# One-hot matrices of the edge stage made by GpSimd and ScalarE in place of VectorE

## What is computed

```python
def _tconv(x, src, dst, edge_attr, ...):
    q, k, v = x @ Wq + bq, x @ Wk + bk, x @ Wv + bv      # (n, H=4, C=64)
    e = edge_attr @ We
    kj, vj = k[src] + e, v[src] + e
    logits = einsum('ehc,ehc->eh', q[dst], kj) / sqrt(C)
    m = segment_max(logits, dst)
    ex = exp(logits - m[dst])
    a = ex / (segment_sum(ex, dst)[dst] + 1e-16)
    return segment_sum(vj * a[:, :, None], dst) + x @ Ws + bs
```

## Time and profile before

| | |
|---|---|
| median of 3 runs | 5051.55 us (5050.83 to 5053.5) |
| profiled execution, its own time | 5044.08 us |
| its span in the trace | 5042.3 us |
| mean granted TensorE clock | 0.933 |
| busy share PE, DVE, ACT, POOL | 83%, 76%, 54%, 54% |
| `edges`, first gather of layer 1 to last of layer 2 | 470.7 to 4046.1 us |

### The profile page before, as it was taken

How to read it: one execution, slowest core, us unless ns; L and a number is a source line. 1 busy time by engine, 2 the same in 40 slices (tenths; PEclk the granted TensorE clock), 3 DMA queues, 4 the chain that set the end, 5 groups by cost and what they waited for, 6 DMA issues and landing times. The chain is left out here.

```text
span 5042.3 us, 107396 instructions
## 1 busy us (share of the span) xinstructions
PE 4191.8 (83%) x19200; PEld 3376.1 (67%) x19201; DVE 3851.4 (76%) x8465; ACT 2724.1 (54%) x10172; POOL 2738.1 (54%) x2848
## 2 busy tenths in 40 slices
PE   2986999999999999978899999999999943049960
PEld 1555888788778788733688878877877833049960
DVE  3444999999999999955799999999999977202222
ACT  0120677777777777731477777767777741013320
POOL 1011777667667677500677767766767723442235
PEclk9998999999999999999999999999999975579985
DMA  4457877777777777534877777777777723522235
GB/s 85 138 195 225 235 215 215 212 216 215 209 212 216 209 217 216 170 118 143 233 219 215 217 209 215 213 210 212 217 213 214 216 74 104 175 94 70 71 95 152
DMA packets 616287, 920.13 MB, mean 182 GB/s; under 512 B 114501, under 2 KB 477829, under 8 KB 615558
## 3 DMA queue, kind: packets, MB, share of 16 engines
q0 software_dynamic: 154448, 501.87, 34.8%
q1 hardware_dynamic: 378390, 323.25, 22.5%
q10 hardware_dynamic: 82848, 88.64, 4.9%
HBM read 800.89 MB, written 112.53 MB: 181 GB/s over the span
## 5 line engine op out<-in xcount | busy, mean ns | idle before, releaser
L870 POOL DMA_INDIRECT edge_kv<-kvD,edge_ix x1760 | 1821.9, 1035 | 961.9 <-issue 556.5
L909 ACT ACTIVATE edge_w<-edge_vj,edge_ex 128x64 f32<-128x64 f32 x7040 | 1872.0, 340 | 647.3 <-PE edge_pa L950 377.1
L927 PE MATMUL edge_ps<-edge_We,edge_ea 112*128 112x256 f32 x7040 | 1842.4, 384 | 52.3 <-DVE edge_prod L1062 19.0
L927 PEld LDWEIGHTS edge_ps<-edge_We,edge_ea 112*128 112x128 f32 x7040 | 1326.9, 191 | 294.0 <-issue 63.6
L950 PE MATMUL edge_pa<-edge_w,edge_oh 128*128 128x260 f32 x3520 | 1095.5, 393 | 122.2 <-DVE acc L984 94.0
L931 PE MATMUL edge_ps<-acc,edge_oht 128*128 x3520 | 1057.8, 381 | 0.3 <-issue 0.3
L950 PEld LDWEIGHTS edge_pa<-edge_w,edge_oh 128*128 128x128 f32 x3520 | 618.2, 189 | 325.3 <-ACT edge_w L911 165.5
L984 DVE TENSOR_TENSOR acc<-acc,edge_pa 128x260 f32 x1760 | 733.0, 416 | 99.2 <-PE edge_pa L950 46.9
L931 PEld LDWEIGHTS edge_ps<-acc,edge_oht 128*128 128x128 f32 x3520 | 675.0, 192 | 96.5 <-issue 1.7
L1030 DVE TENSOR_TENSOR edge_kj<-edge_kv,edge_ps 128x512 f32<-128x512 f32 x880 | 599.1, 681 | 52.3 <-PE edge_ps L931 23.2
L1062 DVE TENSOR_TENSOR edge_prod<-edge_kj,edge_ps 128x512 f32<-128x512 f32 x880 | 598.9, 681 | 0.0
(11 more groups left out here) (228 smaller groups left out, 3194.7 us busy)
## 6 DMA issues: line engine op xcount, KB each, us to landing
edge_ea<-ea_t_dram SPq DMA_DIRECT2D x1760, 112.0 KB
edge_kb<-relD SPq DMA_DIRECT2D x178, 160.0 KB
edge_kv<-kvD,edge_ix POOLq DMA_INDIRECT x1760
kvD<-nodes_kvs ACTq DMA_DIRECT2D x98, 256.0 KB
exp_xr<-xsD SPq DMA_DIRECT2D x105, 128.0 KB
ysD<-exp_yo ACTq DMA_DIRECT2D x105, 128.0 KB
xsD<-mix_zr POOLq DMA_DIRECT2D x26, 512.0 KB
edge_pen<-penD SPq DMA_DIRECT2D x352, 32.0 KB
```

What stands on the lines that cost most here:

```text
L870: nc.gpsimd.indirect_dma_start(out=kv[:, j % HT, :], out_offset=None, in_=g.kvD, in_offset=bass.IndirectOffsetOnAxis(ap=ix[:, h, j % HT:j ...
L909: nc.scalar.activation(w[:, j % 4, h * CA:h * CA + C], vj[:, slot, h * C:(h + 1) * C], ACT.Copy, scale=ex[:, x, h, k:k + 1])
L927: nc.tensor.matmul(ps[:, j % 4, 0:D], ea[:, j % HT, k, :], We[:, k, :], start=(k == 0), stop=(k == 1))
```

## The change

VectorE no longer makes `oh`. GpSimd writes `free - relS` into `oh` (new function `offsets`), ahead of its gathers of steps 5 and 14; ScalarE takes Abs of it in place and then Relu(1 - that) (new function `onehot`), at its steps 3 and 16. The value is the same: 1 where the difference is 0, and 0 elsewhere. TensorE waits for `s_ohs`, which ScalarE raises, in place of `s_oh`. The wait for `s_ape` moves from VectorE to GpSimd. ScalarE's `keyed` for the odd half moves from its step 4 to 6.

```diff
@@ GpSimd
+            def offsets(m, par):
+                need(pool, s_ape, HT * m - HT)
+                nc.gpsimd.tensor_tensor(oh[:, par, :, :], g.free[:, :].unsqueeze(1).to_broadcast([P, HT, P]),
+                                        g.relS[:, bass.ds(m * HT, HT)].unsqueeze(2).to_broadcast([P, HT, P]), ALU.subtract).then_inc(s_off, 1)
+
             def chunk(c, k0, u, kept, more):
                 p = k0 % 2
                 for j in range(T):
                     h = j // HT
+                    if j == 14 and lagged(c, 16):
+                        offsets(2 * c - 2, 0)
+                    if j == 5 and lagged(c, 6):
+                        offsets(2 * c - 3, 1)
@@ ScalarE
+            def onehot(done, par):
+                act.wait_ge(s_off, done)
+                nc.scalar.activation(oh[:, par, :, :], oh[:, par, :, :], ACT.Abs).then_inc(s_abs, 1)
+                act.wait_ge(s_abs, done)
+                nc.scalar.activation(oh[:, par, :, :], oh[:, par, :, :], ACT.Relu, bias=g.ones[:, 0:1], scale=-1.0).then_inc(s_ohs, 1)
+
             def chunk(c, k0, u, kept, more):
                 p = k0 % 2
                 for j in range(T):
-                    if j == 4 and main(c):
+                    if j == 3 and lagged(c, 6):
+                        onehot(2 * c - 2, 1)
+                    if j == 16 and lagged(c, 16):
+                        onehot(2 * c - 1, 0)
+                    if j == 6 and main(c):
                         keyed(2 * c + 1, c, 1)
@@ TensorE
                         if j % HT == 6:
-                            pe.wait_ge(s_oh, 2 * c - (2 if j < HT else 1))
+                            pe.wait_ge(s_ohs, 2 * c - (2 if j < HT else 1))
@@ VectorE
-            def onehot(m, par):
-                need(dve, s_ape, HT * m - HT)
-                nc.vector.tensor_tensor(oh[:, par, :, :], g.free[:, :].unsqueeze(1).to_broadcast([P, HT, P]),
-                                        g.relS[:, bass.ds(m * HT, HT)].unsqueeze(2).to_broadcast([P, HT, P]), ALU.is_equal).then_inc(s_oh, 1)
...
-                    if j % HT == 0 and lagged(c, j + 6):
-                        onehot(2 * c - (3 if j < HT else 2), 1 if j < HT else 0)
```

More of the change, by code:

```diff
@@ L785, in edges @@
             st.sem(n) for n in ("s_we", "s_np", "s_far", "s_oht", "s_ix", "s_step", "s_spare", "s_zero", "s_none", "s_pe", "s_kj", "s_vj", "s_prod", "s_red"))
-        s_oh, s_w, s_ape, s_acc, s_init = (st.sem(n) for n in ("s_oh", "s_w", "s_ape", "s_acc", "s_init"))
-        s_resc, s_vinit, s_off, s_abs = (st.sem(n) for n in ("s_resc", "s_vinit", "s_off", "s_abs"))
+        s_w, s_ape, s_acc, s_init = (st.sem(n) for n in ("s_w", "s_ape", "s_acc", "s_init"))
+        s_resc, s_vinit, s_off, s_abs, s_ohs = (st.sem(n) for n in ("s_resc", "s_vinit", "s_off", "s_abs", "s_ohs"))
         s_mt, s_m, s_D, s_et, s_ex, s_Y = (st.sem(n) for n in ("s_mt", "s_m", "s_D", "s_et", "s_ex", "s_Y"))
```

## The result

The changed kernel takes 5216.5 us (median of 4, 5204.4 to 5227.6) against 5051.2 us before (4 runs, 5049.6 to 5053.5): a ratio of 1.0329, 95% interval 1.0311 to 1.0346. It is slower by 165 us, outside the range on record. The profiled execution's span is 5219.9 us against 5042.3 us, 177.6 us more.

What follows compares the result with a forecast made beforehand. VectorE and TensorE were taken as full before, GpSimd as the bound after (37.6 us mean chunk against 37.77). Loop -7 us, fill +1.8, drain +7.6 a layer, +5 for two layers, gave 5056 us against 5051.6; range 5005 to 5160.

Steps and rivals of the forecast that it cites:

- rival 3: In the loop, GpSimd's step-14 subtraction stalls VectorE's X scan (L1038), 2.1 us a chunk, 5125 us; chance 0.13.
- the sum: Whole kernel: loop -7 us, fill +1.8, drain +7.6, together +2.4 us a layer, +5 for two.
- Subtraction at 2.8 us: GpSimd, twice a chunk: each subtraction of 1,280 values takes 2.8 us; wrong if outside 2.6 to 3.0.
- GpSimd sets the pace at 37.1 us: In the loop, GpSimd's unhindered 31.5 us plus 5.6 for two subtractions bounds the chunk at 37.1 us.
- TensorE's floor at 35.7 (34.7 to 36.2): In the loop, TensorE keeps its work, loses its waits and needs 35.7 us a chunk, between 34.7 and 36.2.
- VectorE at 34.2 us without its one-hots: In the loop, VectorE loses two one-hots of 1.48 us, going from 37.15 to 34.2 us a chunk.
- ScalarE fits: In the loop, ScalarE's busy time rises 5.5 us to 33.2 us a chunk and fits, if its order fits.
- rival 4: ScalarE is late for TensorE at step 16 of the chunk; with one us late, 5140 us; chance 0.10.
- Drain +7.6 us a layer: At a layer's end ScalarE sets the pace and gets three one-hots of 2.7 us, adding 7.6 us.
- Rival 1: In the loop, a subtraction below 2.1 us lets TensorE set the pace, 36.3 us a chunk, 4945 us; chance 0.12.
- Rival 2: In the loop, the subtraction costs 3.6 us each, making 39.1 us a chunk, 5186 us; chance 0.15.

Runs made afterwards that it cites:

- run 1: Changed kernel, GpSimd's step-5 subtraction made to wait until VectorE's rescaling of the chunk before is done: 5029.6 us, ratio 0.995.
- run 2: Changed kernel with the rescaling's factors `fn` written by ScalarE to PSUM, leaving the rescaling one SBUF input: 5030.6 us, ratio 0.9942.
- run 11: Changed kernel with VectorE's rescaling moved one instruction earlier, ahead of the reduction before it: 4984.3 us, ratio 0.991.
- run 3: Kernel before, plus GpSimd's two subtractions at steps 5 and 14 into a tile nobody reads: 5279.9 us, ratio 1.0457.
- run 4: Kernel before, plus GpSimd's two subtractions into an unread tile, the first at step 8 instead of 5: 5207.9 us, ratio 1.0298.
- run 7: Changed kernel with no one-hot made in the loop, `oh` set to zero once before it: 4859.9 us, ratio 0.9665.
- run 12: Changed kernel with VectorE's rescaling moved two instructions earlier, ahead of the product and reduction before it: 4985.7 us, ratio 0.9912.
- run 8: run 1 with the one-hots of each layer's last two chunks made by VectorE again: 4988.7 us, ratio 0.9913.
- run 6: Changed kernel with only the earlier half moved (steps 5 and 3), VectorE making the other half's one-hot: 5257.9 us, ratio 1.0448.

## Why the prediction was wrong, point by point

**The step that failed is in rival 3:** "At the full lead of ten steps nothing meets: the subtraction of step 5 would start at 1213.85 + 0.95 = 1214.80, behind L1021 of 1214.49." The place was right to 0.01 us: 0.31 predicted, 0.32 measured. The conclusion wasn't: a VectorE instruction with two SBUF inputs that starts 0.3 us before GpSimd's is held to its end, so they do meet, in 75 of 88 chunks, at 2.54 us each, a cost that the sum put at nothing. Runs 1, 2 and 11 take the stall away in three ways (later subtraction, PSUM input, earlier rescaling) and each lands at 0.991 to 0.995; run 3 makes it without the rest. The rival had the mechanism and gave it 0.13, through the wrong instruction (L1038). It also let the subtraction of step 14 end 0.6 us ahead of L1038 and left out the clearing COPY that follows at once, which holds the X scan in runs 1, 4 and 11. The Trainium skill, SBUF - State Buffer, section "SBUF: two separate sides", says that of two such instructions the one that starts first gets the shared ports and the other is blocked. By that rule the rescaling would have run through in 0.42 us; the trace disagrees where the starts are 0.3 us apart (2.96 us). It agrees from 0.7 us on: in the kernel before, a one-hot that starts 0.76 us ahead of a COPY (2652.43) takes its 1.48 us, and the COPY is the one that takes longer, 1.63 us instead of 1.06.

**Subtraction at 2.8 us:** 2.33 us, below the range of 2.6 to 3.0. If the operation of the earlier trace rows is of the same kind, the two sizes give an estimate of (2.33 - 0.72) / 1024 = 1.6 ns a value and a fixed part of 0.3 us. 2 x 0.47 = 0.9 us a chunk too much. The Trainium skill's figure (GPSIMD Engine Reference, section 3.1) led to the same 2.8, and the trace disagrees with it by as much.

**GpSimd sets the pace at 37.1 us:** wrong for the changed kernel, where GpSimd waits 122 us for `vj` and 99 for `s_ape`. The mechanism was right and its size off for the kernels without the stall: with 2.33 us it is 31.5 + 4.7 = 36.2, and run 11's chunk is 36.15. In the changed kernel VectorE's stall sets the pace, TensorE's waits with it.

**TensorE's floor at 35.7 (34.7 to 36.2):** inside its bounds, 35.2 (run 7).

**VectorE at 34.2 us without its one-hots:** right (34.0 in run 7), but only while nothing holds it; 34.2 + 2.5 for the rescaling is already 36.7. TensorE is late by its wait of 1.78 us behind the stall, and VectorE later waits for TensorE in turn (1.42 us before a `kj` at 1309.61), some 2.2 us a chunk together, which makes 38.9.

**ScalarE fits (rival 4):** right. With both one-hots on it the chunk is 36.2 us in run 11; in the changed kernel TensorE waits 0.49 us for it at one step.

**Drain +7.6 us a layer:** 10 to 11, mis-sized; ScalarE pays nearly all of the three one-hots, and the first subtraction stands behind a clearing that the last `vj` releases (ScalarE waits 5.06 us there in layer 1):

```profile
2202.12 1.05 POOL L868 COPY acc<-edge_zero 128x1040 f32 x1 [14.15 <-DVE edge_vj L1056]
```

```profile
2205.49 1.27 ACT L899 ACTIVATE edge_oh<-edge_oh 128x1280 f32<-128x1280 f32 x1 [5.06 <-POOL edge_oh L852]
```

**Rival 1 (a cheap subtraction, 36.3 us, 4945 us)** is close to what the change does without the rescaling's stall: the median chunk of runs 11 and 12 is 36.2 us. But its subtraction had to be below 2.1 us, and what bounds those runs is GpSimd. Its time isn't reached there (ratio 0.991, against 4945 / 5051.6 = 0.979), since their mean chunk is 36.5 to 36.7 instead of 36.3 and the drain costs more than it allowed.

**Rival 2 (5186 us)** comes nearest to the measured time, and its chunk of 39.1 us to the measured 39.4, by luck: the subtraction that it needed at 3.6 us took 2.33.

What stays open: why the hold reaches back, and its exact edge. Over all traces, behind a gather and without a wait of GpSimd's own, an instruction was held at up to 0.67 us ahead (an X scan in run 1) and free from 0.64 us on in some cases and from 0.71 us on in all. Where GpSimd waited for the rescaling itself, as in run 1, 0.50 us was free.

## What to carry to other kernels

Work moved to GpSimd is priced first by what it meets, then by its length: list every VectorE instruction with two SBUF inputs, and let each start 0.9 us or more before a GpSimd operation, or behind its end; merely started first is not enough. Add up GpSimd's own chunk as well, since it is the next bound (36.2 us here). When a GpSimd instruction is added or moved, all later ones shift, old ones too, so list the meetings again for all of them. Where two meet, exchange neighbours in VectorE's order or put one input into PSUM; each was worth about 4% here.

## What the runs showed of the hardware

- A VectorE instruction with two SBUF inputs is held by a GpSimd operation whose recorded start lies up to 0.6 us behind its own (rescaling at 0.32 us, one-hot at 0.21, B scan at 0.60), even where it would have ended 0.1 us before that start. It then ends behind GpSimd's end by its own length less 0.1 to 0.2 us (rescaling 0.31 of 0.42 us, B scan 0.30 of 0.47, one-hot 1.36 of 1.48, X scan 0.07 of 0.25). From 0.71 us ahead it isn't held, and at 0.76 us the longer one-hot held the COPY instead (1.63 us against 1.06).
- GpSimd's one-input COPY holds it like a two-input subtraction. Of 309 such instructions over all traces that started beside one GpSimd operation with another right behind it, 301 were held through both (run 8, 1263.02: an X scan of 2.27 us). The other 8 lie in the drains of runs 3 and 4, where for instance a one-hot ran between a subtraction and a COPY (run 3, 2242.18: 2.19 us, and the COPY 2.31).
- Instructions with one SBUF input and one in PSUM (products, additions, the rescaling of run 2) and the reduction run beside either at their usual length.
- After TensorE's waits of 0.86 and 2.08 us the granted clock was 0.84 over the next 10 us in one chunk of run 6 and 1.00 in the one before it, which is 1.7 us a chunk between such chunks; after the single wait of 1.78 us in the changed kernel's chunk it stayed at 1.00.
